# One exponent search per weight tile instead of one per pair, and one quantization in eight on VectorE instead of one in four

## The chip, the cores and the metric

The kernel runs on the 8 cores of one Trainium2 chip. Every core works on 1024 of the 8192 tokens and on all the weights, and the cores do not talk to each other. The metric is the device time of the slowest core in microseconds (us). Times and profile below are of one profiled execution; the profile is of the slowest core, core 2.

## The reference

The reference is one transformer layer: a linear attention with a residual and a layer norm, and then a feed-forward part whose three matrix products take operands in a block format ("MX").

```python
def _quantize_elem(x, ebits, mfrac, max_norm):
    ax = jnp.abs(x)
    priv = jnp.floor(jnp.log2(jnp.where(ax == 0, 1.0, ax)))
    priv = jnp.maximum(priv, float(-2 ** (ebits - 1) + 2))
    scale = jnp.exp2(priv - mfrac)
    return jnp.clip(jnp.round(x / scale) * scale, -max_norm, max_norm)

def _quantize_mx(x, ebits, mfrac, emax_elem, max_norm):
    # blocks of 32 along the last axis
    amax = jnp.max(jnp.abs(xb), axis=-1, keepdims=True)
    sexp = jnp.floor(jnp.log2(jnp.where(amax == 0, 1.0, amax))) - emax_elem
    scale = jnp.exp2(sexp)
    return (_quantize_elem(xb / scale, ...) * scale).reshape(shp)

gate = q_act(x) @ q_w(w_gate).T      # x: tokens x 2048, w_gate, w_up: 8192 x 2048
up = q_act(x) @ q_w(w_up).T
out = q_act(silu(gate) * up) @ q_w(w_down).T     # w_down: 2048 x 8192
x = layernorm(x + out)
```

So every weight and every activation is divided by a power of two that is found per block of 32, rounded to a few bits, and multiplied back, before TensorE sees it as bf16.

## The kernel before

After the attention (to about 490 us) the 8 activation tiles of 128 tokens are quantized (the XQ part, width 2048). Then a loop runs over 16 slabs of 512 of the 8192 inner columns. In a slab four kinds of work follow each other: the weights `wd` (of the slab before), `wg` and `wu` are loaded and quantized; the down product of the slab before is made and added to `BIG2` (`down_section`); the gate and up products are made, and the four pieces of `INTER` are quantized; then `wd` is pushed. A slab has 4 tiles of 128 x 2048 of each weight, 12 in all, which are handled as 6 pairs. I call an uninterrupted run of pairs a weight phase: there are 17, the first of 4 pairs (`wg`, `wu`), 15 of 6 pairs, and the last of 2 (`wd`).

A pair goes through `wq_back`. It quantizes the four half tiles q0 to q3 (128 x 1024) that wait in `WST`, and after q1 and after q3 it loads one tile of the next pair into the slot just read and reduces it to 64 block maxima (`p.red` into PSUM tile `PSC`, line 563). At the start of `wq_back` stands the exponent search for the two tiles together, 128 blocks wide (`emit_search`, line 573): one scaling, one memset, 5 steps of three dependent VectorE instructions, one scaling, one reciprocal. In a step the first instruction reads `PSC` in PSUM and one SBUF tile (s_c<-scw,PSC), the second and third have two SBUF inputs (s_c<-s_c,scw and scw<-scw,s_c).

`emit_quant` (line 234) quantizes one half tile. I call its parts head, middle and tail.

- Head: multiply by the inverse scale and clamp (lines 252, 254), on GpSimd ("gp") or on VectorE ("dve"), whichever `QPAT` names. Then ScalarE squares the result (line 255).
- Middle: always three VectorE instructions (lines 256 to 259: INTER<-fmd, fmd<-fmd, fmd<-INTER,fmd; WST<-fmd in place of INTER<-fmd when activations are quantized).
- Tail: add, subtract, multiply by the scale into `WQN` (lines 269 to 271), on the engine of the head, and then the transposing DMA from `WQN` on the SP queue. The tail of a half tile is emitted only after the middle of the next one (`tmp["pend"]`), so on GpSimd the order is head of k+1, tail of k, head of k+2, tail of k+1.

`QPAT = (0, 1, 1, 1)` puts every fourth quantization on VectorE. A slab has 28 of them (24 weight halves, 4 pieces of `INTER`), so each pair starts with one on VectorE, and so does each group of four `INTER` pieces; q1, q2, q3 are on GpSimd. `WQN` is one buffer: whoever writes it waits for the transposing DMA that still reads it. Every engine runs its own queue in program order; semaphores connect them.

Of the kernel before, what the change touches and what calls it, by code (L numbers as in the profile page):

```python
# [157 lines left out]
def r3(ap, w=32):  # L158
    return ap.rearrange("p (b w) -> p b w", w=w)


def build_program():
# [20 lines left out]
    with ExitStack() as stG:  # L183
# [28 lines left out]
        def emit_search(amax_ap, keys_amax, q_ap, kq, qi_ap, kqi, t_ap, kt, c_ap, kc, f_ap):  # L212
            n = c_ap.shape[1]
            ka = list(keys_amax)
            p.ts(amax_ap, amax_ap, SEARCH_PRE, None, Alu.mult, None, ka, ka)
            p.memset(q_ap, 1.0, [kq])
            for b in SEARCH_STEPS:
                p.stt(c_ap, q_ap, float(2.0 ** b), amax_ap, Alu.mult, Alu.is_le,
                      [kq] + ka, [kc])
                p.stt(c_ap, c_ap, float(2.0 ** b - 1.0), q_ap, Alu.mult, Alu.mult,  # L220
                      [kc, kq], [kc])
                p.tt(q_ap, q_ap, c_ap, Alu.add, [kq, kc], [kq])
            p.ts(q_ap, q_ap, SEARCH_POST_S, None, Alu.mult, None, [kq], [kq])
            p.recip(qi_ap, q_ap, [kq], [kqi])

        QC = [0]
        QPAT = (0, 1, 1, 1)

        def flushq(tmp):
            if tmp["pend"] is not None:  # L230
# [3 lines left out]
        def emit_quant(src_ap, src_keys, inv_bc, scale_tile_ap, blk0, scale_keys,  # L234
                       out_ap, out_keys, kc_col, hi, tmp, tasp, post=()):
            k = QC[0]
            QC[0] += 1
            se = "gp" if QPAT[k % len(QPAT)] else "dve"
            par = tmp["p" + se]
# [61 lines left out]
        with ExitStack() as stA:  # L301
# [92 lines left out]
            for tt in range(2):  # L394
                for hc in range(HC):
                    slot = hc % 2
# [116 lines left out]
        with ExitStack() as stF:  # L513
            sf = lambda n, shp, dt=F32: stF.enter_context(nc.sbuf_tensor(n, shp, dt))
# [3 lines left out]
            WDT = sf("WDT", [128, NQT * H], BF16)  # L518
            WST = sf("WST", [128, H * 2])
            WQN = sf("WQN", [128, H // 2], BF16)  # L520
            scw = sf("scw", [128, 256])
            invw = sf("invw", [128, 256])
            s_c2 = sf("s_c2", [128, 128])
            wpc = [0]
            igc = [0]
            PSC = pf("PSC", [128, 160])
            am_w = PSC[:, 0:128]
            am_i = PSC[:, 128:160]
            INTER = sf("INTER", [128, 4 * ISLAB])
# [15 lines left out]

            def wq_load_tile(dram, s, ti, kind):
                slot = ti % 2
                wst = WST[:, slot * H:(slot + 1) * H]
                if kind == "d":
                    srcap = wd.rearrange("(c p) i -> p c i", p=128)[  # L550
                        :, :, s * ISLAB + ti * 128: s * ISLAB + (ti + 1) * 128]
                    dstw = wst.rearrange("p (c i) -> p c i", i=128)
                    p.dma("act", f"d_ws{slot}", dstw[:, 0:8, :], srcap[:, 0:8, :],
                          reads=[f"wst{slot}a"], writes=[f"wst{slot}a"])
                    p.dma("act", f"d_ws{slot}x", dstw[:, 8:16, :], srcap[:, 8:16, :],
                          reads=[f"wst{slot}b"], writes=[f"wst{slot}b"])
                else:
                    srcap = dram[s * ISLAB + ti * 128: s * ISLAB + (ti + 1) * 128, :]
                    p.dma("act", f"d_ws{slot}", wst[:, 0:1024], srcap[:, 0:1024],
                          reads=[f"wst{slot}a"], writes=[f"wst{slot}a"])  # L560
                    p.dma("act", f"d_ws{slot}x", wst[:, 1024:2048], srcap[:, 1024:2048],
                          reads=[f"wst{slot}b"], writes=[f"wst{slot}b"])
                p.red(am_w[:, slot * 64:(slot + 1) * 64].unsqueeze(2), r3(wst), Alu.max,
                      [f"wst{slot}a", f"wst{slot}b"], [f"amw{slot}"], absval=True)

            def wq_back(job, nxt):
                dram, s, t0, kind, wkey = job
                wpar = wpc[0] % 2
                wpc[0] += 1
                scwS = scw[:, wpar * 128:(wpar + 1) * 128]  # L570
                invwS = invw[:, wpar * 128:(wpar + 1) * 128]
                skeys = [f"scw{wpar}", f"invw{wpar}"]
                emit_search(am_w[:], ["amw0", "amw1"], scwS, skeys[0], invwS, skeys[1],
                            None, "wt2", s_c2[:], "wc2", None)
                for idx, ti in enumerate((t0, t0 + 1)):
                    slot = ti % 2
                    wst = WST[:, slot * H:(slot + 1) * H]
                    for hh in range(2):
                        kst = f"wst{slot}" + ("b" if hh else "a")
                        c0 = slot * 64 + hh * 32  # L580
                        ib = invwS[:, c0:c0 + 32].unsqueeze(2).broadcast_to([128, 32, 32])
                        if kind == "d":
                            dst = WDT[:, ti * H + hh * 1024: ti * H + (hh + 1) * 1024
                                      ].rearrange("p (c j) -> p c j", j=128)
                        else:
                            buf = WGT if kind == "g" else WUT
                            dst = buf[:].rearrange("p (c i) -> p c i", i=ISLAB)[
                                :, hh * 8:(hh + 1) * 8, ti * 128:(ti + 1) * 128]

                        def post_w(_dst=dst, _sem={"g": "d_trg", "u": "d_tru",  # L590
                                                   "d": "d_trd"}[kind], _wk=wkey):
                            p.dma("sp", _sem, _dst, WQN[:], reads=["wqn"], writes=[_wk],
                                  transpose=True)
                        emit_quant(wst[:, hh * 1024:(hh + 1) * 1024], [kst], ib, scwS, c0,
                                   skeys, WQN[:], ["wqn"],
                                   7, CLAMP_W, tmpw,
                                   (INTER[:, 0:1024], ["int_0", "int_1"],
                                    INTER[:, 1024:2048], ["int_2", "int_3"]),
                                   post=(post_w,))
                    if nxt is not None:  # L600
                        wq_load_tile(nxt[0], nxt[1], nxt[2] + idx, nxt[3])

            def wq_push(job):
                if WPEND[0] is None:
                    for idx in range(2):
                        wq_load_tile(job[0], job[1], job[2] + idx, job[3])
                else:
                    wq_back(WPEND[0], job)
                WPEND[0] = job

            def wq_flush_pipe():
                if WPEND[0] is not None:
                    wq_back(WPEND[0], None)
                    WPEND[0] = None
# [161 lines left out]
```

How the kernel before makes its waits and increments, by code:

```python
        def go(h, _w=tuple(waits), _b=build, _hs=hsem, _inc=inc):  # L90
            for hs, v in _w:
                h.wait_ge(hs, v)
            ins = _b(h)
            if _hs is not None:
                ins.then_inc(_hs, _inc)
# [9 lines left out]
    def wait_raw(self, eng, sem, val):  # L105
        hs = self.semh[sem]
        self.ops[eng].append(lambda h, _hs=hs, _v=val: h.wait_ge(_hs, _v))
```

## Time and profile before

| | us |
|---|---|
| median of 3 runs | 7727.88 (7724.46 to 7749.57) |
| the profiled execution, its own time | 7723.47 |
| its span on core 2 | 7721.8 |
| spans of all cores | 7703.4 to 7721.8 |
| VectorE (DVE) busy | 5589.4 |
| GpSimd (POOL) busy | 3811.9 |
| TensorE (PE) busy | 1603.0 |

The profile names the engines PE, DVE, ACT (ScalarE), POOL (GpSimd) and SP; L122 and the like are lines of helpers that record each operation, so operations are told apart by the tiles they write and read. A time in a timeline is the start in us from the start of the span; an instruction that waits inside the engine for access to memory counts as busy, so a duration can be longer than the work. An engine's idle time stands in square brackets with what ended it.

### The profile page before, as it was taken

What the parts mean: (1) busy time and instruction counts of PE and PEld (TensorE: products, weight loads), DVE (VectorE), ACT (ScalarE), POOL (GpSimd) and SP (SyncE); (2) the same over time, 40 slices, a digit from 0 to 9 for tenths busy, and PEclk for the clock granted to TensorE, in tenths of its full rate; (3) what the DMA queues carried; (4) which work ended last, traced back from release to release, by engine and by line L of the source; (5) the groups of instructions that cost most, each with busy time, mean ns of one, the idle gap of its engine ahead of it and who ended that gap; (6) DMA issues with size and microseconds to landing.
All of it is one profiled execution on the core that took longest, in us unless ns stands there. A gap on an engine that the chain in (4) does not pass through costs nothing.

```text
span 7721.8 us, 36833 instructions; the slowest of 8 cores (7703.4 to 7721.8 us)
## 1 busy us (share of the span) xinstructions
PE 1603.0 (21%) x6690; PEld 708.9 (9%) x6816; DVE 5589.4 (72%) x6491; ACT 591.1 (8%) x634; POOL 3811.9 (49%) x1730
## 2 busy tenths in 40 slices
PE   4400302204040301204040402204040402204041
PEld 2100100001010100101010100001010100001010
DVE  3387677686868777686868777786868777786867
ACT  0010000000000000000000000000000000000001
POOL 0036455463636455464636455463636465463633
PEclk7555656657575655657575655657575756657575
DMA  3001121221112121111112121111212121111201
GB/s 110 0 8 48 34 61 40 48 52 36 58 31 57 32 61 41 47 52 36 59 30 61 29 62 40 48 53 36 60 27 63 28 61 40 48 53 36 63 25 65
DMA packets 670360, 354.97 MB, mean 46 GB/s; under 512 B 499121, under 2 KB 630578, under 8 KB 668978
## 3 DMA queue, kind: packets, MB, share of 16 engines
q10 hardware_dynamic: 169984, 201.35, 8.4%
q1 hardware_dynamic: 496818, 134.49, 7.7%
q0 software_dynamic: 3328, 16.78, 0.7%
q14 instruction: 173, 1.42, 0.1%
q8 instruction: 57, 0.93, 0.1%
HBM read 222.50 MB, written 8.39 MB: 30 GB/s over the span
## 4 chain that ended last, share of the span: by engine, by line
DVE 53%; issue 12%; PE 11%; POOL 11%; DMA 7%; ACT 4%; DVEq 1%; ACTq 1%; POOLq 0%; another core or an unknown queue 0%; SPq 0%
DVE fy L122 8%; DVE s_c L130 7%; PE psY L148 7%; DVE fmd L127 6%; DVE INTER L127 5%; DVE fmd L130 4%; DVE scw L122 4%; DVE PSC L139 3%; ACT fmd L144 3%; DVE WQN L122 3%; DVE fy L127 3%; POOL WQN L122 3%; POOL fy L122 2%; DMA WST<-wd 2%; POOL INTER L122 2%
## 5 line engine op out<-in xcount | busy, mean ns | idle before, releaser
L148 PE MATMUL psY<-WDT,INTQF 128*128 128x512 bf16 x2006 | 502.6, 414 | 5252.4 <-DVE BIG L122 2884.5
L122 POOL TENSOR_TENSOR fy<-fy,fmd 128x1024 f32<-128x1024 f32 x336 | 878.0, 2613 | 440.3 <-DVE fmd L130 412.1
L122 POOL TENSOR_TENSOR INTER<-INTER,fmd 128x1024 f32<-128x1024 f32 x288 | 765.1, 2656 | 332.5 <-DVE fmd L130 307.4
L127 DVE TENSOR_SCALAR INTER<-fmd 128x1024 f32<-128x1024 f32 x384 | 498.2, 1298 | 584.6 <-ACT fmd L144 574.4
L130 DVE SCALAR_TENSOR_TENSOR fmd<-INTER,smalls,fmd 128x1024 f32<-128x1024 f32 x384 | 747.3, 1946 | 43.4 <-DVE fmd L127 1.8
L148 PEld LDWEIGHTS psY<-WDT,INTQF 128*128 128x128 bf16 x2048 | 211.8, 105 | 5543.1 <-issue 5342.3
L127 DVE TENSOR_SCALAR fmd<-fmd,smalls 128x1024 f32<-128x1024 f32 x448 | 572.9, 1279 | 50.5 <-DVE INTER L127 2.8
L144 ACT ACTIVATE fmd<-fy 128x1024 f32<-128x1024 f32 x280 | 290.5, 1054 | 4122.1 <-DVE fy L127 2635.9
L139 DVE TENSOR_REDUCE PSC<-WST 128x64 f32<-128x2048 f32 x192 | 438.3, 2283 | 205.5 <-DMA WST<-wd 177.8
L122 POOL TENSOR_TENSOR fy<-WST,invw 128x1024 f32<-128x1024 f32 x144 | 356.4, 2475 | 440.2 <-DVE invw L136 429.2
L122 POOL TENSOR_TENSOR INTER<-WST,invw 128x1024 f32<-128x1024 f32 x144 | 356.2, 2474 | 385.6 <-DVE invw L136 374.9
L148 PE MATMUL psU<-WUT,XQF 128*128 128x512 bf16 x1024 | 408.4, 399 | 572.5 <-DMA WUT<-WQN 486.7
L122 DVE TENSOR_TENSOR fy<-fy,fmd 128x1024 f32<-128x1024 f32 x224 | 460.8, 2057 | 13.7 <-DVE fmd L130 0.5
L122 DVE TENSOR_TENSOR BIG<-BIG,psY 128x512 f32<-128x512 f32 x512 | 349.8, 687 | 109.8 <-PE psY L148 97.6
L122 POOL TENSOR_TENSOR WQN<-fy,scw 128x1024 bf16<-128x1024 f32 x144 | 304.8, 2117 | 213.8 <-DVE INTER L127 62.1
L122 POOL TENSOR_TENSOR WQN<-INTER,scw 128x1024 bf16<-128x1024 f32 x144 | 303.8, 2110 | 214.1 <-DVE INTER L127 58.2
L148 PE MATMUL psG<-WGT,XQF 128*128 128x512 bf16 x984 | 391.3, 398 | 0.0
L148 PE MATMUL psY<-WUT,XQF 128*128 128x512 bf16 x1024 | 388.7, 380 | 2.1
L148 PE MATMUL psY<-WGT,XQF 128*128 128x512 bf16 x983 | 372.9, 379 | 0.0
L122 POOL TENSOR_TENSOR WST<-INTER,invi 128x1024 f32<-128x1024 f32 x24 | 45.9, 1911 | 554.6 <-DVE invi L136 554.6
L122 POOL TENSOR_TENSOR fy<-INTER,invi 128x1024 f32<-128x1024 f32 x24 | 45.8, 1910 | 543.6 <-DVE invi L136 543.6
L122 DVE TENSOR_TENSOR WQN<-fy,scw 128x1024 bf16<-128x1024 f32 x96 | 297.2, 3096 | 17.5 <-DVE fy L122 15.9
(170 smaller groups left out, 4087.9 us busy)
## 6 DMA issues: line engine op xcount, KB each, us to landing
WST<-wg ACTq DMA_DIRECT2D x128, 512.0 KB, 4.0
WST<-wu ACTq DMA_DIRECT2D x128, 512.0 KB, 4.1
WST<-wd ACTq DMA_DIRECT2D x128, 512.0 KB, 5.1
xps<-xP POOLq DMA_DIRECT2D x8, 1024.0 KB, 7.2
BIG<-xT SPq DMA_DIRECT2D x16, 512.0 KB, 18.8
y<-BIG POOLq DMA_DIRECT2D x8, 1024.0 KB, 4.2
WGT<-WQN SPq DMA_TRANSPOSE x128, 2.7
WUT<-WQN SPq DMA_TRANSPOSE x128, 2.7
```

The costliest lines, as they stand in the source:

```text
L122: return self.emit(eng, lambda h: h.tensor_tensor(out, a, b, op), reads, writes)
L127: return self.emit(eng, lambda h: h.tensor_scalar(out, a, s1, s2, op1, op2), reads, writes)
L130: return self.emit(eng, lambda h: h.scalar_tensor_tensor(out, a, s, b, op1, op2), reads, writes)
L139: return self.emit("dve", lambda h: h.tensor_reduce(out, a, AX, op, apply_absolute_value=absval), reads, writes)
L144: return self.emit("act", lambda h: h.activation(out, a, func, bias=bias, scale=scale), reads, writes)
L148: return self.emit("pe", lambda h: h.matmul(out, lhsT, rhs, start=start, stop=stop), reads, writes, quiet=quiet)
```

## The change

The search moves from the start of `wq_back` into `wq_load_tile`, right behind the reduction of each tile: two searches of 64 blocks in place of one of 128. The scales get three slots of 64 instead of two of 128, and `TSL` keeps which tile has which slot. `QPAT` gets a period of 8 with one zero.

```diff
-        QPAT = (0, 1, 1, 1)
+        QPAT = (0, 1, 1, 1, 1, 1, 1, 1)
...
-            scw = sf("scw", [128, 256])
-            invw = sf("invw", [128, 256])
+            scw = sf("scw", [128, 192])
+            invw = sf("invw", [128, 192])
...
             def wq_load_tile(dram, s, ti, kind):
                 slot = ti % 2
+                sl3 = wtc[0] % 3
+                wtc[0] += 1
+                TSL[(kind, s, ti)] = sl3
...
                 p.red(am_w[:, slot * 64:(slot + 1) * 64].unsqueeze(2), r3(wst), Alu.max,
                       [f"wst{slot}a", f"wst{slot}b"], [f"amw{slot}"], absval=True)
+                emit_search(am_w[:, slot * 64:(slot + 1) * 64], [f"amw{slot}"],
+                            scw[:, sl3 * 64:(sl3 + 1) * 64], f"scw{sl3}",
+                            invw[:, sl3 * 64:(sl3 + 1) * 64], f"invw{sl3}",
+                            None, "wt2", s_c2[:, 0:64], "wc2", None)
 
             def wq_back(job, nxt):
                 dram, s, t0, kind, wkey = job
-                emit_search(am_w[:], ["amw0", "amw1"], scwS, skeys[0], invwS, skeys[1],
-                            None, "wt2", s_c2[:], "wc2", None)
                 for idx, ti in enumerate((t0, t0 + 1)):
                     slot = ti % 2
+                    sl3 = TSL.pop((kind, s, ti))
+                    skeys = [f"scw{sl3}", f"invw{sl3}"]
+                    scwS = scw[:, sl3 * 64:(sl3 + 1) * 64]
+                    invwS = invw[:, sl3 * 64:(sl3 + 1) * 64]
```

VectorE, the part of a pair from its first tail on, before (fy is the VectorE half tile q0, the L127 and L130 rows are middles, PSC<-WST is the reduction of the tile just loaded):

```order
L122 TENSOR_TENSOR fy<-fy,fmd 128x1024 x2
L122 TENSOR_TENSOR WQN<-fy,scw 128x1024
L139 TENSOR_REDUCE PSC<-WST 128x64
L127 TENSOR_SCALAR INTER<-fmd 128x1024
L127 TENSOR_SCALAR fmd<-fmd,smalls 128x1024
L130 SCALAR_TENSOR_TENSOR fmd<-INTER,smalls,fmd 128x1024
```

The same place on VectorE in the changed kernel:

```order
L122 TENSOR_TENSOR fy<-fy,fmd 128x1024 x2
L122 TENSOR_TENSOR WQN<-fy,scw 128x1024
L139 TENSOR_REDUCE PSC<-WST 128x64
L126 TENSOR_SCALAR PSC<-PSC 128x64
L155 MEMSET scw 128x64
L130 SCALAR_TENSOR_TENSOR s_c<-scw,PSC 128x64
L130 SCALAR_TENSOR_TENSOR s_c<-s_c,scw 128x64
L122 TENSOR_TENSOR scw<-scw,s_c 128x64
```

The search now stands between the reduction and the middle of q2. The start of a pair on VectorE before, from the end of its search:

```order
L126 TENSOR_SCALAR scw<-scw 128x128
L136 RECIPROCAL invw<-scw 128x128
L122 TENSOR_TENSOR fy<-WST,invw 128x1024
L127 TENSOR_SCALAR fy<-fy 128x1024
L127 TENSOR_SCALAR INTER<-fmd 128x1024
L127 TENSOR_SCALAR fmd<-fmd,smalls 128x1024
L130 SCALAR_TENSOR_TENSOR fmd<-INTER,smalls,fmd 128x1024
```

And on VectorE in the changed kernel, in every second pair:

```order
L126 TENSOR_SCALAR scw<-scw 128x64
L136 RECIPROCAL invw<-scw 128x64
L127 TENSOR_SCALAR INTER<-fmd 128x1024
L127 TENSOR_SCALAR fmd<-fmd,smalls 128x1024
L130 SCALAR_TENSOR_TENSOR fmd<-INTER,smalls,fmd 128x1024
```

The VectorE head has gone from it, and so has the tail; the pairs between them still have both. On GpSimd, where a head writes from WST and invw, before, across the border of two pairs (two tails in a row, then two heads in a row):

```order
L122 TENSOR_TENSOR INTER<-INTER,fmd 128x1024 x2
L122 TENSOR_TENSOR WQN<-INTER,scw 128x1024
L122 TENSOR_TENSOR fy<-fy,fmd 128x1024 x2
L122 TENSOR_TENSOR WQN<-fy,scw 128x1024
L122 TENSOR_TENSOR INTER<-WST,invw 128x1024
L127 TENSOR_SCALAR INTER<-INTER 128x1024
L122 TENSOR_TENSOR fy<-WST,invw 128x1024
L127 TENSOR_SCALAR fy<-fy 128x1024
```

And on GpSimd in the changed kernel, in and into a pair that is all on GpSimd:

```order
L122 TENSOR_TENSOR INTER<-WST,invw 128x1024
L127 TENSOR_SCALAR INTER<-INTER 128x1024
L122 TENSOR_TENSOR fy<-fy,fmd 128x1024 x2
L122 TENSOR_TENSOR WQN<-fy,scw 128x1024
L122 TENSOR_TENSOR fy<-WST,invw 128x1024
L127 TENSOR_SCALAR fy<-fy 128x1024
L122 TENSOR_TENSOR INTER<-INTER,fmd 128x1024 x2
L122 TENSOR_TENSOR WQN<-INTER,scw 128x1024
```

Heads and tails alternate there without a break, since the scales of the next tile are known half a pair earlier.

## Rows read from the trace of the kernel before

**Rows 1.** The page: busy time of an engine, and the chain that ended last
```profile
PE 1603.0 (21%) x6690; PEld 708.9 (9%) x6816; DVE 5589.4 (72%) x6491; ACT 591.1 (8%) x634; POOL 3811.9 (49%) x1730
...
DVE 53%; issue 12%; PE 11%; POOL 11%; DMA 7%; ACT 4%; DVEq 1%; ACTq 1%; POOLq 0%; another core or an unknown queue 0%; SPq 0%
```

**Rows 2.** Timeline of DVE, one pair: start, duration, engine, line, operation, [idle before]
```profile
3242.35 1.23 DVE L122 TENSOR_TENSOR fy<-WST,invw 128x1024 f32<-128x1024 f32 x1
...
3247.15 2.18 DVE L127 TENSOR_SCALAR INTER<-fmd 128x1024 f32<-128x1024 f32 x1 [1.25 <-ACT fmd L144]
...
3252.28 0.69 DVE L127 TENSOR_SCALAR INTER<-fmd 128x1024 f32<-128x1024 f32 x1
...
3255.15 4.50 DVE L122 TENSOR_TENSOR fy<-fy,fmd 128x1024 f32<-128x1024 f32 x2
...
3262.85 2.28 DVE L139 TENSOR_REDUCE PSC<-WST 128x64 f32<-128x2048 f32 x1
...
3273.72 1.65 DVE L127 TENSOR_SCALAR INTER<-fmd 128x1024 f32<-128x1024 f32 x1 [4.29 <-ACT fmd L144]
...
3280.89 2.28 DVE L139 TENSOR_REDUCE PSC<-WST 128x64 f32<-128x2048 f32 x1
```

**Rows 3.** Timeline of POOL, the same pair and the start of the next
```profile
3255.38 6.46 POOL L122 TENSOR_TENSOR INTER<-INTER,fmd 128x1024 f32<-128x1024 f32 x2 [5.15 <-DVE fmd L130]
3265.97 2.37 POOL L122 TENSOR_TENSOR WQN<-INTER,scw 128x1024 bf16<-128x1024 f32 x1 [4.13 <-DVE INTER L127]
...
3271.36 1.04 POOL L127 TENSOR_SCALAR INTER<-INTER 128x1024 f32<-128x1024 f32 x1 [0.16 <-POOL INTER L122]
3272.47 5.09 POOL L122 TENSOR_TENSOR fy<-fy,fmd 128x1024 f32<-128x1024 f32 x2
...
3281.10 4.83 POOL L122 TENSOR_TENSOR INTER<-INTER,fmd 128x1024 f32<-128x1024 f32 x2 [1.22 <-DVE fmd L130]
3286.07 1.91 POOL L122 TENSOR_TENSOR WQN<-INTER,scw 128x1024 bf16<-128x1024 f32 x1
3294.40 2.96 POOL L122 TENSOR_TENSOR fy<-WST,invw 128x1024 f32<-128x1024 f32 x1 [6.42 <-DVE invw L136]
```

**Rows 4.** Timeline of DVE, the search that follows, beside the POOL rows above
```profile
3284.26 1.81 DVE L130 SCALAR_TENSOR_TENSOR s_c<-s_c,scw 128x128 f32<-128x128 f32 x1
3286.18 1.95 DVE L122 TENSOR_TENSOR scw<-scw,s_c 128x128 f32<-128x128 f32 x1
3288.24 0.29 DVE L130 SCALAR_TENSOR_TENSOR s_c<-scw,PSC 128x128 f32<-128x128 f32 x1
```

**Rows 5.** Timeline of DVE, the 32-wide search of INTER while POOL has a tail
```profile
3150.77 1.95 DVE L122 TENSOR_TENSOR sci<-sci,s_c 128x32 f32<-128x32 f32 x1
```

**Rows 6.** Timeline of DVE, first and next instruction around a 128-wide and a 32-wide search
```profile
684.96 0.30 DVE L126 TENSOR_SCALAR PSC<-PSC 128x128 f32<-128x128 f32 x1
...
692.93 1.23 DVE L122 TENSOR_TENSOR fy<-WST,invw 128x1024 f32<-128x1024 f32 x1
...
3094.77 0.20 DVE L126 TENSOR_SCALAR PSC<-PSC 128x32 f32<-128x32 f32 x1
...
3100.33 1.23 DVE L122 TENSOR_TENSOR fy<-INTER,invi 128x1024 f32<-128x1024 f32 x1
```

**Rows 7.** Timeline of DVE, start of a weight phase, and what follows its end
```profile
3176.62 2.29 DVE L139 TENSOR_REDUCE PSC<-WST 128x64 f32<-128x2048 f32 x1 [12.16 <-DMA WST<-wd]
...
3190.34 1.23 DVE L122 TENSOR_TENSOR fy<-WST,invw 128x1024 f32<-128x1024 f32 x1
...
3488.03 0.68 DVE L122 TENSOR_TENSOR BIG<-BIG,psY 128x512 f32<-128x512 f32 x1
```

**Rows 8.** Timeline of POOL, XQ part
```profile
611.14 12.90 POOL L122 TENSOR_TENSOR ln_scr<-ln_scr,qmd 128x2048 f32<-128x2048 f32 x2 [3.68 <-DVE qmd L130]
...
639.39 10.96 POOL L122 TENSOR_TENSOR qy<-qy,qmd 128x2048 f32<-128x2048 f32 x2 [2.29 <-DVE qmd L130]
650.50 5.50 POOL L122 TENSOR_TENSOR XQ<-qy,sc_x 128x2048 bf16<-128x2048 f32 x1
```

More of the change, by code:

```diff
@@ L520, in build_program @@
             WQN = sf("WQN", [128, H // 2], BF16)
-            scw = sf("scw", [128, 256])
-            invw = sf("invw", [128, 256])
+            scw = sf("scw", [128, 192])
+            invw = sf("invw", [128, 192])
             s_c2 = sf("s_c2", [128, 128])
-            wpc = [0]
             igc = [0]
+            wtc = [0]
+            TSL = {}
             PSC = pf("PSC", [128, 160])
@@ L564, in wq_load_tile @@
                       [f"wst{slot}a", f"wst{slot}b"], [f"amw{slot}"], absval=True)
+                emit_search(am_w[:, slot * 64:(slot + 1) * 64], [f"amw{slot}"],
+                            scw[:, sl3 * 64:(sl3 + 1) * 64], f"scw{sl3}",
+                            invw[:, sl3 * 64:(sl3 + 1) * 64], f"invw{sl3}",
+                            None, "wt2", s_c2[:, 0:64], "wc2", None)
             def wq_back(job, nxt):
                 dram, s, t0, kind, wkey = job
[L568 to L572, printed above, removed]
-                emit_search(am_w[:], ["amw0", "amw1"], scwS, skeys[0], invwS, skeys[1],
-                            None, "wt2", s_c2[:], "wc2", None)
                 for idx, ti in enumerate((t0, t0 + 1)):
                     slot = ti % 2
+                    sl3 = TSL.pop((kind, s, ti))
+                    skeys = [f"scw{sl3}", f"invw{sl3}"]
+                    scwS = scw[:, sl3 * 64:(sl3 + 1) * 64]
+                    invwS = invw[:, sl3 * 64:(sl3 + 1) * 64]
                     wst = WST[:, slot * H:(slot + 1) * H]
@@ L579, in wq_back @@
                         kst = f"wst{slot}" + ("b" if hh else "a")
-                        c0 = slot * 64 + hh * 32
+                        c0 = hh * 32
                         ib = invwS[:, c0:c0 + 32].unsqueeze(2).broadcast_to([128, 32, 32])
```

## The prediction, written before the changed kernel had run

> **What bounds the kernel now.** I read the page first. VectorE is busy 72% and GpSimd 49% of the span, and VectorE has 53% of the chain that ended last [rows 1]. Then the timeline of one pair in a weight phase, on both engines. It is the same pair over and over: the VectorE head starts at 3242.35 [rows 2] and the next one with the GpSimd head at 3294.40 [rows 3], so a pair takes 52.0 us; 96 pairs are some 5000 of the 7722 us. What the reader is to see there is that the two engines take turns at something. A GpSimd multiply takes 1.91 us alone [rows 3], and 2.96 where a VectorE multiply of 1.23 has begun just before it [rows 2, 3]. A VectorE instruction of the middle takes 0.69 when GpSimd is idle, and the same one 2.18 when it isn't [rows 2]. In the search, s_c<-s_c,scw lasts 1.81 us in place of 0.29: it ends 0.14 after the GpSimd tail's second instruction (3285.93), and the next, scw<-scw,s_c, starts 0.1 too late, after the next GpSimd multiply has begun at 3286.07, and ends 0.15 behind that one [rows 3, 4]. s_c<-scw,PSC, with one operand in PSUM, takes 0.29. So each VectorE instruction that reads two SBUF tiles (or is a tensor_scalar on SBUF) waits for the whole GpSimd instruction that runs, and between two GpSimd instructions only one gets through. The second of such a couple is blocked in 78 places of the 128-wide search, and in 32 of the 32-wide one [rows 5], so shorter instructions don't slip through either.
>
> The Trainium skill states this as a rule ("SBUF — State Buffer", Who interferes with whom): VectorE and GpSimd share a pair of ports under an exclusive lock, held for the instruction, and the loser blocks fully. By that rule instructions that only shared bandwidth would not exist, and the trace agrees (1.81 for 0.29); it speaks against this change, which gives GpSimd more instructions and VectorE more short ones that need the lock.
>
> **The change, part by part.** Terms: a GpSimd head is 1.91 + 0.16 + 1.04 = 3.1 us, a tail 4.83 + 0.14 + 1.91 = 6.9 [rows 3], with the gap 10.1 per half tile. A middle on VectorE alone is 3.0 (3252.28 to about 3255.2) [rows 2]. Beside a running GpSimd tail it is 7.2 (3273.72 to 3280.89) [rows 2] and holds GpSimd up by 1.7; starting together with the tail, about 6.9.
>
> A search: 7.97 us for 128 blocks (684.96 to 692.93), 5.56 for 32 (3094.77 to 3100.33) [rows 6]. A 64-wide one isn't in the trace; it lies between the two, and a third of the way is 6.35, or 0.32 per instruction. For a 64-element fp32 instruction the Trainium skill ("VectorE: DVE Perf Modes", The TRN2 errata) has an estimate of (64 + 151)/0.96 = 224 ns plus the gap, which gives the same 0.32; the rows at 128 and 32 fit that form. Two of 64 in place of one of 128 are 4.7 us more per pair even alone. Of a search's 19 instructions 11 need the lock (two per step, and the last scaling).
>
> Pair all on GpSimd (every second one). Let 0 be the end of VectorE's middle of q1 (or q3). GpSimd then has 8 instructions that wait for no VectorE work: the last 1.8 us of a tail, a head, a tail, a head, ending at 15.2 (1.8 + 3.1 + 6.9 + 3.1 and gaps). VectorE reduces to 2.4, and starts the search; blocked once per GpSimd instruction, its lock instructions end at 3.9, 5.1, 7.6, 10.1, 12.1, 14.1 and 15.3. Four steps are nearly through when GpSimd stalls; four instructions of 0.32, the scaling and the reciprocal end at 17.6. Now the middle of the next half tile, alone: 20.6. Only here can GpSimd go on with its tail, and the other middle beside it ends at 27.5. Two such halves are 55.0.
>
> Pair with q0 on VectorE. Head and square 4.8 (3242.35 to 3247.15 [rows 2]); middles of q0 and q1 alone 6.0, against 8.0 before, because GpSimd has made the head of q1 already (its scales came half a pair earlier): 2 us gained. The tail of q0 beside the tail of q1 takes 7.8 as before (3255.15 to 3262.85 [rows 2]), sum 18.6. GpSimd waits 4.1 for `WQN` there, as before [rows 3]. Reduction and search stand next: the search meets that multiply (1.91) and the head of q3, three GpSimd instructions, and ends 12.4 after the tail. Before, VectorE made the middle of q2 in this time and then idled 4.3 for the head of q3 [rows 2]; that idle time goes, and is covered. Then middles 3.0 and 6.9, and reduction and second search under the GpSimd run of 8 instructions, 17.6: sum 58.4. When the next pair starts on VectorE there are only 6 GpSimd instructions to run (to 12.0), and that last term is 15.3: so the all-GpSimd pair before it takes 52.6.
>
> Against 52.0: +6.4 for 40 pairs of the one kind, +0.6 for 39 of the other, together +279. The last pair of each of the 17 phases has no loads and no searches; from the end of its search it took 37.3 (five pairs of 52.1 after 3190.34, to 3488.03 [rows 7]) and now, stepped in the same way, 35.5 or 35.0: -35. The starts: 13.7 from the first reduction to the first head (3176.62 to 3190.34 [rows 7]); now reduce, search, reduce, search, 17.5 where the first pair has a VectorE head (9 times), and 19.4 where GpSimd already runs two heads through the second search (8 times): +80. Sum of the weight phases +324.
>
> The `INTER` groups: a head on GpSimd in place of one on VectorE gives the group back 2.4 us and costs the next group's search 2.7 [rows 5]; nothing. XQ part: one of two VectorE tiles goes to GpSimd, which is the busy engine there. It adds a tail (10.96 + 0.15 + 5.50) and a head of about 7, 24 us, less the waits of 3.7 and 2.3 that it fills [rows 8]: +18, between 0 (if the VectorE tile that goes had been on the path for as long) and +24. Loads: a tile is asked for when its slot's second head and square are done, 11 us or more before the reduction; hidden. Scale slots: three are enough for two tiles in use and one in the making; no wait.
>
> Sum +342. The profiled execution's own time of 7723.5 becomes 8065; it lies 4.4 under the median of the runs shown, so 8070. Bounds: if no GpSimd instruction blocked a search, a pair would cost 4.7 more and gain 2.0 and up to 4.3, between -1.6 and +2.7 per pair; if nothing overlapped, a pair would be GpSimd's 47 (below) and two searches and two middles alone, 12.7 + 6.0, together 66, +14. The stepped value lies at +3.5 on average because GpSimd stalls for want of middles before the search is through. An error of 1.3 us per pair is 125 us.
>
> **Rivals.**
> The search vanishes beside GpSimd (faster). Place: the two searches of a pair. If two lock instructions pass at every border of GpSimd instructions, a search ends before GpSimd stalls; then a pair all on GpSimd takes its 40.4 plus 4 x 1.75 that the middles hold it up, 47.4, one with a VectorE head some 51, mean -2.8 per pair, about 7480. It decides from about 9 of 11 lock instructions through by the stall. Against it: in 110 of 110 places the second was blocked. For it: a GpSimd clamp starts 0.16 after the multiply [rows 3], the longest border, and 64-wide instructions are shorter than 128-wide ones.
> The costs cancel (no change to measure): the idle times of 4.3 on VectorE and 6.4 on GpSimd per pair [rows 2, 3] take up both the extra search and the blocking. 7690 to 7780.
> It costs more: a GpSimd that is never idle also delays every tail of VectorE, and the loads, asked for later beside steadier transposes, come late at a reduction by 2 or 3 us (they had 8 us before without a wait). 8150 to 8300.
>
> **How the numbers follow.** Forecast 8070 with its own range 7930 to 8150: 0.76. More costly: 0.09, all slower. Costs cancel: 0.08, of which 0.03 faster, 0.03 within 0.3% (23 us, about what a measurement here can tell from none) and 0.02 slower. Search hidden: 0.07, faster. So faster 0.10, same 0.03, slower 0.87. The range is the forecast's own with a little of the costlier case, 7930 to 8160.
>
> **What would show it.** Right: 64-wide s_c<-s_c,scw and scw<-scw,s_c with means near 1 us where 0.22 is the bare time; pairs alternating near 58 and 53 us; GpSimd idle before fy<-fy,fmd and INTER<-INTER,fmd with the releaser VectorE fmd in every half pair, some 5 us; no idle time before heads. Wrong in the first step: those means under 0.5. Wrong in the second: VectorE idle before the first middle instruction as long as now. Wrong as a whole: the mean pair at or under 52.

## The result, and the profile after

The changed kernel takes 7996.5 us (median of 8 runs, 7993.5 to 8008.6) against 7723.6 before; the ratio of the runs is 1.0353 (95% interval 1.034 to 1.0367). It is slower by 273 us. The forecast was 8070, range 7930 to 8160.

The page after, the parts that answer to [rows 1]:

```profile
span 7993.2 us, 40881 instructions; the slowest of 8 cores (7978.8 to 7993.2 us)
...
PE 1628.0 (20%) x6816; PEld 711.5 (9%) x6816; DVE 6046.5 (76%) x8030; ACT 591.0 (7%) x634; POOL 4251.8 (53%) x2015
...
DVE 59%; issue 17%; PE 10%; POOL 7%; DMA 2%; ACT 2%; DVEq 2%; ACTq 0%; POOLq 0%; SPq 0%
```

Both vector engines are busy for longer: VectorE by 457 us, though it lost half of its heads and tails, and GpSimd by 440. Where VectorE's time went stands in the groups of the changed kernel (xcount, busy us, mean ns, idle before and its releaser):

```profile
L122 DVE TENSOR_TENSOR scw<-scw,s_c 128x64 f32<-128x64 f32 x960 | 821.9, 856 | 102.9 <-DVE s_c L130 3.9
L130 DVE SCALAR_TENSOR_TENSOR s_c<-s_c,scw 128x64 f32<-128x64 f32 x960 | 744.3, 775 | 105.9 <-DVE s_c L130 7.0
...
L130 DVE SCALAR_TENSOR_TENSOR s_c<-scw,PSC 128x64 f32<-128x64 f32 x960 | 212.5, 221 | 103.9 <-DVE scw L122 3.9
```

The three are the same size and do much the same work. The last one, with its PSUM operand, takes 221 ns; the two with both operands in SBUF take 775 and 856. Before, those two were 528.6 us busy together (480 each); now 1566.2. Of the instructions of these two kinds, 158 of 960 took over 0.4 us before, and 883 of 1920 do now. Each of the 883 ends 72 to 87 ns behind the end of a GpSimd instruction, and no two of them behind the same one (before: 146 to 150 ns, all 158, and again no two behind the same one).

A half of a pair that is all on GpSimd, first on VectorE:

```profile
3357.50 2.28 DVE L139 TENSOR_REDUCE PSC<-WST 128x64 f32<-128x2048 f32 x1
...
3360.68 0.80 DVE L130 SCALAR_TENSOR_TENSOR s_c<-s_c,scw 128x64 f32<-128x64 f32 x1
3361.58 1.09 DVE L122 TENSOR_TENSOR scw<-scw,s_c 128x64 f32<-128x64 f32 x1
...
3363.10 2.00 DVE L130 SCALAR_TENSOR_TENSOR s_c<-s_c,scw 128x64 f32<-128x64 f32 x1
3365.20 2.37 DVE L122 TENSOR_TENSOR scw<-scw,s_c 128x64 f32<-128x64 f32 x1
...
3368.36 1.27 DVE L130 SCALAR_TENSOR_TENSOR s_c<-s_c,scw 128x64 f32<-128x64 f32 x1 [0.46 <-DVE s_c L130]
3369.74 1.95 DVE L122 TENSOR_TENSOR scw<-scw,s_c 128x64 f32<-128x64 f32 x1
...
3372.11 0.76 DVE L130 SCALAR_TENSOR_TENSOR s_c<-s_c,scw 128x64 f32<-128x64 f32 x1
3372.98 0.23 DVE L122 TENSOR_TENSOR scw<-scw,s_c 128x64 f32<-128x64 f32 x1
...
3375.06 0.63 DVE L127 TENSOR_SCALAR INTER<-fmd 128x1024 f32<-128x1024 f32 x1
...
3378.06 0.69 DVE L127 TENSOR_SCALAR INTER<-fmd 128x1024 f32<-128x1024 f32 x1
...
3384.70 2.28 DVE L139 TENSOR_REDUCE PSC<-WST 128x64 f32<-128x2048 f32 x1
```

The same stretch on GpSimd:

```profile
3359.49 1.91 POOL L122 TENSOR_TENSOR INTER<-WST,invw 128x1024 f32<-128x1024 f32 x1
3361.56 1.04 POOL L127 TENSOR_SCALAR INTER<-INTER 128x1024 f32<-128x1024 f32 x1 [0.16 <-POOL INTER L122]
3362.68 4.82 POOL L122 TENSOR_TENSOR fy<-fy,fmd 128x1024 f32<-128x1024 f32 x2
3367.64 1.91 POOL L122 TENSOR_TENSOR WQN<-fy,scw 128x1024 bf16<-128x1024 f32 x1
3369.70 1.91 POOL L122 TENSOR_TENSOR fy<-WST,invw 128x1024 f32<-128x1024 f32 x1
3371.76 1.04 POOL L127 TENSOR_SCALAR fy<-fy 128x1024 f32<-128x1024 f32 x1 [0.16 <-POOL fy L122]
3378.10 5.59 POOL L122 TENSOR_TENSOR INTER<-INTER,fmd 128x1024 f32<-128x1024 f32 x2 [5.30 <-DVE fmd L130]
```

The reader is to lay one beside the other. From 3359.5 to 3372.8 GpSimd has head, tail, head without a break, and each instruction of VectorE that reads two SBUF tiles ends just behind a GpSimd instruction: seven of them, one after the other. (Below I call these, and a tensor_scalar on SBUF, lock instructions.) At 3372.8 GpSimd has run out: it needs a middle, and the middle stands behind the search. From there the search runs at 0.23 us per instruction, the middle follows, and GpSimd starts again at 3378.10 after 5.30 us. That wait is the new one; before, GpSimd waited 6.42 us for the scales at a pair's start [rows 3]; the scales of a pair's first tile now come early.

The half takes 27.2 us (3357.50 to 3384.70). A pair all on GpSimd takes 51.8 us (3347.86 to 3399.69), and one with a VectorE head, here the one before it, 58.2 (3289.70 to 3347.86):

```profile
3289.70 1.16 DVE L122 TENSOR_TENSOR fy<-WST,invw 128x1024 f32<-128x1024 f32 x1
...
3300.43 4.50 DVE L122 TENSOR_TENSOR fy<-fy,fmd 128x1024 f32<-128x1024 f32 x2
...
3308.13 2.28 DVE L139 TENSOR_REDUCE PSC<-WST 128x64 f32<-128x2048 f32 x1
...
3320.66 0.63 DVE L127 TENSOR_SCALAR INTER<-fmd 128x1024 f32<-128x1024 f32 x1
...
3347.86 0.63 DVE L127 TENSOR_SCALAR INTER<-fmd 128x1024 f32<-128x1024 f32 x1
...
3399.69 1.16 DVE L122 TENSOR_TENSOR fy<-WST,invw 128x1024 f32<-128x1024 f32 x1
```

Over the span, 271.4 us more. The 15 phases of six pairs took 4677 us before and 4926 after (+248.5), each read from its first reduction to the first VectorE instruction of the work behind it. The first and the last phase add 20, and what lies between the phases is 10 less. The first reduction of a weight tile, which ends the XQ part, moved from 679.24 to 692.72 (+13.5).

### The profile page after: what moved, and what is told of

The parts are those of the page before. It is cut to its first block, busy times and chain, and to the rows that moved or that the text cites. A ratio compares the mean times of both kernels' runs of the same rounds, so it can differ in the third digit from the quotient of the medians.

```text
span 7993.2 us, 40881 instructions; the slowest of 8 cores (7978.8 to 7993.2 us)
## 1 busy us (share of the span) xinstructions
PE 1628.0 (20%) x6816; PEld 711.5 (9%) x6816; DVE 6046.5 (76%) x8030; ACT 591.0 (7%) x634; POOL 4251.8 (53%) x2015
## 4 chain that ended last, share of the span: by engine, by line
DVE 59%; issue 17%; PE 10%; POOL 7%; DMA 2%; ACT 2%; DVEq 2%; ACTq 0%; POOLq 0%; SPq 0%
DVE s_c L130 14%; DVE scw L122 10%; DVE fmd L127 7%; PE psY L148 7%; DVE PSC L139 6%; DVE fmd L130 4%; DVE fy L122 4%; DVE INTER L127 3%; DVEq L92 2%; ACT fmd L144 2%; POOL fy L122 2%; DVE sci L122 2%; DVE fy L127 1%; POOL WST L122 1%; POOL INTER L122 1%
## 5 line engine op out<-in xcount | busy, mean ns | idle before, releaser
L122 POOL TENSOR_TENSOR fy<-fy,fmd 128x1024 f32<-128x1024 f32 x392 | 1008.3, 2572 | 705.3 <-DVE fmd L130 668.3
L122 POOL TENSOR_TENSOR INTER<-INTER,fmd 128x1024 f32<-128x1024 f32 x336 | 877.8, 2613 | 584.0 <-DVE fmd L130 555.5
L122 DVE TENSOR_TENSOR scw<-scw,s_c 128x64 f32<-128x64 f32 x960 | 821.9, 856 | 102.9 <-DVE s_c L130 3.9
L130 DVE SCALAR_TENSOR_TENSOR s_c<-s_c,scw 128x64 f32<-128x64 f32 x960 | 744.3, 775 | 105.9 <-DVE s_c L130 7.0
L130 DVE SCALAR_TENSOR_TENSOR fmd<-INTER,smalls,fmd 128x1024 f32<-128x1024 f32 x384 | 768.4, 2001 | 45.1 <-DVE fmd L127 1.9
L127 DVE TENSOR_SCALAR fmd<-fmd,smalls 128x1024 f32<-128x1024 f32 x448 | 625.8, 1397 | 49.1 <-DVE INTER L127 0.9
L144 ACT ACTIVATE fmd<-fy 128x1024 f32<-128x1024 f32 x252 | 263.2, 1054 | 3724.4 <-DVE fy L127 1541.1
L127 DVE TENSOR_SCALAR INTER<-fmd 128x1024 f32<-128x1024 f32 x384 | 285.0, 742 | 229.9 <-ACT fmd L144 210.5
L122 POOL TENSOR_TENSOR WQN<-fy,scw 128x1024 bf16<-128x1024 f32 x168 | 375.2, 2233 | 121.0 <-DVE s_c L130 79.1
L122 POOL TENSOR_TENSOR WQN<-INTER,scw 128x1024 bf16<-128x1024 f32 x168 | 375.2, 2233 | 120.7 <-DVE s_c L130 83.2
## 6 DMA issues: line engine op xcount, KB each, us to landing
BIG<-xT SPq DMA_DIRECT2D x16, 512.0 KB, 19.4
```

Of the source, the lines that this page charges most:

```text
L122: return self.emit(eng, lambda h: h.tensor_tensor(out, a, b, op), reads, writes)
L127: return self.emit(eng, lambda h: h.tensor_scalar(out, a, s1, s2, op1, op2), reads, writes)
L130: return self.emit(eng, lambda h: h.scalar_tensor_tensor(out, a, s, b, op1, op2), reads, writes)
L144: return self.emit("act", lambda h: h.activation(out, a, func, bias=bias, scale=scale), reads, writes)
```

## The experiments

Two theories went in. The lock theory: the time is lost where short VectorE instructions wait, one by one, for whole GpSimd instructions, in front of middles that GpSimd needs. The load theory: GpSimd simply got too much work by `QPAT`, or VectorE too many instructions. Each run was timed beside the kernel before; ratios are against it.

### One part of the change alone

```diff
# e1, on the kernel before
-        QPAT = (0, 1, 1, 1)
+        QPAT = (0, 1, 1, 1, 1, 1, 1, 1)
# e2, on the changed kernel
-        QPAT = (0, 1, 1, 1, 1, 1, 1, 1)
+        QPAT = (0, 1, 1, 1)
```

> Edit: the kernel before with only QPAT changed to one zero in eight; the search stays one per pair, 128 wide. Lock theory (the time goes where the search's short VectorE instructions each wait for a whole GpSimd instruction in front of the middles that GpSimd needs): a pair with a VectorE head stays at 52.0 us, a pair all on GpSimd comes to about 54 (head 3.1 and square 1.1 before the first middle, then middles beside tails at 7 each, reductions and search 13.4), so 48 x 2.2 = 105 plus 13.5 for the XQ part: about 7840 us (7800 to 7880). Rival, the load theory (GpSimd got too much work, which is the bulk of the 273 us): near 7990.

> Edit: the changed kernel with QPAT back at one zero in four; only the search is split and moved. Lock theory: every pair then is 18.3 (head to end of the VectorE tail) + 12.6 (reduction and search) + 9.5 (two middles) + 15.1 (reduction and search) = 55.5 us against 52.0; 79 of them +276, starts and ends about +30: about 8030 us (7990 to 8060), slower than the whole change. Load theory: near 7730.

Measured: `QPAT` alone 7931.5 (1.0272, 1.0249 to 1.0295), the split search alone 8003.8 (1.0363, 1.0343 to 1.0383). So the split search does all of the harm by itself; its pairs take 55.3 to 55.5 us in the trace, for a stepped 55.5. Adding `QPAT` to it changes nothing that can be told (1.0353); that it would be slower than the whole change is not borne out. But `QPAT` alone costs 214 us, outside the 7800 to 7880 of the lock theory and nearly twice its 118; my hand-stepped pair was wrong there. The trace of that run, a pair all on GpSimd:

```profile
1633.42 1.91 POOL L122 TENSOR_TENSOR fy<-WST,invw 128x1024 f32<-128x1024 f32 x1 [11.40 <-DVE invw L136]
...
1636.61 5.09 POOL L122 TENSOR_TENSOR INTER<-INTER,fmd 128x1024 f32<-128x1024 f32 x2
...
1648.15 5.09 POOL L122 TENSOR_TENSOR fy<-fy,fmd 128x1024 f32<-128x1024 f32 x2
...
1659.68 5.09 POOL L122 TENSOR_TENSOR INTER<-INTER,fmd 128x1024 f32<-128x1024 f32 x2
```

GpSimd is idle for 11.4 us while the search runs, and then is the bound, with a half tile every 11.54 us (four are 46.1); the pair takes 59.8, and pairs with a VectorE head 48.8. I had let VectorE's middles set the pace (54), and not GpSimd's queue. Blocking in the search is not what costs here: only 78 of its 960 instructions with two SBUF tiles took over 0.4 us, against 158 before. The time goes into a GpSimd that first waits for the scales and then has all four half tiles to do, so the load theory has a part of this run right. The two parts do not add up (214 + 287 would be 501). A likely reason, argued and not tested by itself: with the split the scales of a pair's first tile are known half a pair earlier, which takes away the 11.4 us of waiting that made `QPAT` dear.

### The lock taken away

```diff
-            s_c2 = sf("s_c2", [128, 128])
...
-            PSC = pf("PSC", [128, 160])
+            PSC = pf("PSC", [128, 288])
+            s_c2 = PSC[:, 160:288]
```

The same edit on the changed kernel (e3), on the kernel before (e4), and on the changed kernel with `QPAT` one in four (e5). The instructions, their number and their order stay as they were.

> Edit: the changed kernel with the search's temporary s_c2 in PSUM (128 more columns of the tile PSC), so that no step of a search reads two SBUF tiles. Lock theory: s_c<-s_c,scw and scw<-scw,s_c fall from 0.78 and 0.86 us to 0.25 or less, a reduction with its search from 12.6 to 17.6 down to about 9, GpSimd becomes the bound of a pair all on GpSimd (about 47 us for 55), pairs with a VectorE head about 46 to 50; with the INTER groups 2.7 us less each: 7050 to 7300 us, faster than both kernels. Rival (the extra search hurts by its bare time of 6.3 us, 19 instructions more, wherever its temporary lies): 7950 to 8000.

> Edit: the kernel before with s_c2 in PSUM in the same way. Lock theory: two of a search's instructions were blocked per pair, 1.5 and 1.7 us: 3.1 x 96 = 300 less, and 2.7 for three INTER groups in each of 16 slabs, 130 less: about 7300 us (7260 to 7450). Rival (blocked time is hidden, since GpSimd has work left): 7650 to 7730.

> Edit: split search with its temporary in PSUM and QPAT at one zero in four. Lock theory: with unblocked searches the early scales are a gain, and QPAT matters little (in the run with QPAT in eight both kinds of pair took about 48 us); XQ part 13 us less: 7280 us (7200 to 7350), better than the unsplit search in PSUM (7393). Rival (splitting is a loss of bare time wherever the temporary is, 4.7 us per pair): 7600 or more.

Measured: 7319.6 (0.9501, 0.9443 to 0.9559), 7393.2 (0.9577, 0.9547 to 0.9608) and 7289.4 (0.9439, 0.9383 to 0.9494). The changed kernel gains 677 us from where the search's temporary lies, and now beats the kernel before by 5%. It lies just outside the range that the lock theory gave (7050 to 7300), and far from the rival's 7950 to 8000; e4 and e5 lie inside theirs, and their rivals are out. The groups of the first of these runs:

```profile
L130 DVE SCALAR_TENSOR_TENSOR PSC<-PSC,scw 128x64 f32<-128x64 f32 x960 | 223.6, 233 | 106.1 <-DVE PSC L130 6.9
...
L122 DVE TENSOR_TENSOR scw<-scw,PSC 128x64 f32<-128x64 f32 x960 | 212.4, 221 | 103.6 <-DVE PSC L130 4.8
L127 POOL TENSOR_SCALAR INTER<-INTER 128x1024 f32<-128x1024 f32 x168 | 191.8, 1142 | 26.9 <-POOL INTER L122 26.9
L126 DVE TENSOR_SCALAR scw<-scw 128x64 f32<-128x64 f32 x192 | 184.0, 958 | 20.8 <-DVE scw L122 0.7
```

The two kinds are at 233 and 221 ns, all 1920 of them; 1566 us of busy time have become 436. It was blocking, and not their number or width. With no blocking the split is no loss any more: 7289 split against 7393 unsplit (e5 and e4, same `QPAT`). So the rival that a split costs its bare 4.7 us per pair wherever it lies has fallen. Beside these 1130 us of busy time, the 32-wide searches of `INTER`, whose temporary moved too, lost another 120 (their two instructions went from 407 and 356 ns to 188 and 200). Of these 1250 us 677 came off the clock: some 575 in the weight phases (5290 us in all in the changed kernel, 4714 here) and some 115 between them (1915 and, on core 5 of this run, 1800). The last row shows part of where the rest went. The scaling at a search's end, a tensor_scalar on SBUF, was at 195 ns in the changed kernel, where GpSimd had stalled by then; it takes 958 now, since the search gets to it while GpSimd still works. Middles are longer too: INTER<-fmd has a mean of 1421 ns in this run and 742 in the changed kernel.

### The last blocked instruction of a search

```diff
+                if t_ap is not None and b == SEARCH_STEPS[-1]:
+                    p.tt(t_ap, q_ap, c_ap, Alu.add, [kq, kc], [kt])      # t_ap in PSUM
...
+                p.ts(q_ap, t_ap, SEARCH_POST_S, None, Alu.mult, None, [kt], [kq])
```

> Edit: split search, QPAT one in four, temporary in PSUM, and the sum of the last step written to PSUM too, so that the last scaling reads PSUM and no instruction of a search reads SBUF twice or as tensor_scalar. Lock theory: that scaling falls from 0.59 us to 0.2 (192 of them, 75 us busy), of which a part is on the path: 7220 to 7280 us against 7289. Rival (that scaling is no lock instruction, its 0.59 us has another cause): unchanged, 7290, and its mean stays near 0.6.

Measured: 7284.2 (0.9436, 0.9411 to 0.9461), which can't be told from 7289.4 and lies just outside the lock theory's 7220 to 7280. The instruction did change:

```profile
L126 DVE TENSOR_SCALAR scw<-PSC 128x64 f32<-128x64 f32 x192 | 42.9, 224 | 20.4
```

It fell from 594 to 224 ns (71 us for all 192), so the rival's reason (no lock there) is wrong, and yet the time did not follow. INTER<-fmd, the next lock instruction behind it in half of the cases, went from 798 to 959 ns (384 of them, 62 us). In the other half the VectorE head follows: its multiply fell from 2101 to 1558 ns (96 of them, 52 us less) and its clamp rose from 1378 to 1804 (48 us more, 112 of them). GpSimd's multiply fy<-WST,invw went from 2043 to 2191. So here a blocked instruction right in front of others passed its wait on; what paid was taking apart the chain of ten, each blocked anew.

### The price of the steps

```diff
-                            None, "wt2", s_c2[:, 0:64], "wc2", None)
+                            None, "wt2", s_c2[:, 0:64], "wc2", None, steps=())
```

> Edit: the changed kernel without the five steps in the weight searches (scaling, memset, scaling and reciprocal stay, so every weight block gets the same scale; the text says this is left out). It gives the whole price of the steps. Lock theory: a pair drops from 55 to 45 to 47 us, where GpSimd's own 4 x 11.5 is the bound: 7000 to 7200 us, that is only 100 to 300 us under the run with the temporary in PSUM (7320), so about three quarters of the price of 800 to 1000 us is blocking and not instructions. Rival (bare time counts): the difference to 7320 is 96 x 2 x 4.9 = 940 us, about 6400.

This kernel leaves out the five steps, so every weight block gets the same scale. Measured: 7122.9 (0.921, 0.9156 to 0.9264), inside the lock theory's range; the rival's 6400 is out. All the steps of the weight searches are worth 874 us in the changed kernel. The 677 us of e3 can't be set beside this as they are, because e3 took the blocking out of the `INTER` searches too. In the traces the weight phases shrink by 877 us here (5290 to 4413) and by some 575 in e3: about two thirds of the price of the steps go when their operands move and the steps stay, and not the three quarters that I expected. Pairs take 48 us (all on GpSimd) and 44; their mean is 46, what four half tiles took GpSimd in e1.

### The place of the search

```diff
                         emit_quant(...)
+                        if late[0] is not None:
+                            late[0]()
+                            late[0] = None
```

> Edit: the changed kernel (QPAT one in eight, temporary in SBUF) with each 64-wide search emitted behind the middle of the next half tile instead of ahead of it. Lock theory, stepped: the search then meets GpSimd's head and tail again (5 blocked instructions), GpSimd runs out because the next tile's head now waits for the scales, and a half pair takes 29 to 33 us in place of 27.2: slower than the change, 8150 to 8600. Rival (the harm is only that the search stands ahead of the middle, and GpSimd starves for that): faster than the change, 7700 to 7900.

`late[0]` holds the search of the tile loaded before. Measured: 8028.1 (1.0406, 1.0371 to 1.0441), about 32 us over the changed kernel, where the ratio's intervals (1.034 to 1.0367 and 1.0371 to 1.0441) just part. The rival said 7700 to 7900 and is out: the search behind the middle is blocked as before (s_c<-s_c,scw 816 ns, scw<-scw,s_c 699), and what GpSimd no longer waits for middles it waits for scales: its idle time before weight heads with invw as the releaser is 555 us in place of 374, and the one before tails with fmd 1094 in place of 1224. Pairs take 57.3 and 53.4 us, a mean of 55.4 for 55.0. My own figure (8150 to 8600) was far too high. It is the blocking that costs; these two places in the queue differ little.

### Half of the work on VectorE

```diff
-        QPAT = (0, 1, 1, 1, 1, 1, 1, 1)      # on e3
+        QPAT = (0, 1)
```

> Edit: as the changed kernel with the temporary in PSUM, QPAT (0, 1): half of the quantizations on VectorE. Both engines hold the shared memory access in turn; a VectorE quantization holds it for less time (5.6 us of head and tail) than a GpSimd one (9.6), but VectorE is then in line with 24 more us per pair. Lock theory with VectorE as the bound: slower than 7320, 7350 to 7700. Rival (GpSimd is the bound, so relief pays): under 7200.

Measured: 7712.4 (0.9987, 0.9959 to 1.0015), just outside the lock theory's range (7350 to 7700): 393 us slower than e3. The rival's figure, under 7200, is out. Pairs take 51.3 us, GpSimd is busy 33% of the span, and it idles 1997 us before tails with VectorE's fmd as the releaser: even without the lock in its search VectorE has no room for a second head and tail per pair. One in four (7289) and one in eight (7320) can't be told apart: their intervals overlap.

## Why the prediction was right

- **What bounds the kernel.** That the two engines take turns at memory, whole instruction by whole instruction, was the ground of it; e3, e4 and e5 show it for the search by taking only the second SBUF operand away. As the Trainium skill says ("SBUF — State Buffer", Who interferes with whom), a VectorE instruction with two SBUF inputs contends with a GpSimd instruction that reads SBUF, and one with at most one SBUF input does not; with that rule the traces agree, 775 and 856 ns against 221 to 233.
- **One lock instruction per border of two GpSimd instructions.** Right, and it was what decided: the rival in which 64-wide instructions slip through needed 9 of 11 done by GpSimd's stall; the trace shows 7, all blocked, one by one, until the stall at 15.3 us (stepped 15.2). (The "110 of 110" of the forecast has an exception in the kernel before: at 2850.24 a second one got through, where GpSimd had paused for 0.43 us.) The half pair came out at 27.2 for a stepped 27.5.
- **64-wide search.** 0.22 us per instruction and 0.33 from start to start, for an estimated 0.32.
- **The pairs.** 51.8 and 58.2 us for 52.6 and 58.4. The 0.8 between 52.6 and 51.8 is a search that I let end at 15.3 and that ended at 15.0, and twice two middles of 9.9 that took 9.6. Over the 15 phases of six pairs this is the main term that was mis-sized: 301 us forecast for them, 248.5 measured. Some 13 of these 52 us lie in the kernel before, whose phases are 4677 us and not the 4665 of my 52.0, 37.3 and 13.7.
- **The last and first pairs.** 35.1 and 34.8 from the last search's end for 35.5 and 35.0; starts 17.3 and 19.4 for 17.5 and 19.4.
- **The XQ part.** +9 for +18, half of the forecast: from the start of the reciprocal inv_x<-sc_x to the first reduction of a weight tile it is 175.6 us before and 184.6 after (means of the 8 cores). `QPAT` does it: 184.8 in e1 and 175.6 in e2. The rest of the 13.5 read above lies ahead of it, where the cores of one run differ by as much.
- **`INTER` groups, loads, scale slots at nothing.** What lies between the phases became 10 us shorter. I have not taken it apart; the cause of these 10 us stays open.
- **Signs named beforehand.** Means "near 1 us where 0.22 is the bare time": 0.78 and 0.86. Pairs near 58 and 53: yes. GpSimd idle some 5 us before a tail with fmd as releaser: 5.30, and 6.59 and 7.27 in the pair with a VectorE head. "No idle time before heads" is wrong for pairs with a VectorE head: there the head of q2 waits for the second search, 5.45 us in the first pair of the phase shown (3289.94) and 3.48 in the third (3399.92).

What the forecast did not see is that either part is a loss alone and that together they are hardly more than one. It stepped only the combination, pair kind by pair kind. That the total came out near is not proof that such stepping can be trusted: in the same way I got 118 us for `QPAT` alone, which costs 214, and 8150 to 8600 for the search behind the middle, which takes 8028. Of the 342 us forecast, 273 came; the terms that were too large are the pairs and the XQ part.

## What to carry to other kernels

When VectorE and GpSimd both work from SBUF, count the short VectorE instructions with two SBUF operands that run while GpSimd is busy: each can cost what is left of a GpSimd instruction, up to 2.4 us here, and not its own 0.2 us, and splitting a chain in two makes more of them. Put a chain's temporary in PSUM before moving, splitting or sharing out the work; here this alone was worth 4.2% on the kernel before and 8.5% on the changed one, and the fastest version (e9 and e5, 5.6% under the kernel before) has it together with the split search and `QPAT` one in four. And step the schedule of the combination: the two parts' prices, 214 and 287 us, do not add.

## What the runs showed of the hardware that was not expected

A VectorE chain that alternates SBUF and PSUM operands ran at the pace of one that is undisturbed (221 to 233 ns per 64-wide instruction) beside a GpSimd that was busy 57% of the span. No two blocked instructions of the weight searches ended behind the same GpSimd instruction, in 883 places; the gap to the next GpSimd instruction there was mostly 0.08 to 0.16 us. Taking the lock from one instruction directly ahead of others moved its wait of 0.37 us to its neighbours and gained nothing that could be measured (7284.2 and 7289.4).
